# Two sets of accumulators by period, and one sum for three layers

## What is computed

```python
for i in range(3):
    z = jnp.einsum('bmd,bnd->bmnd', x, hidden).reshape(B, -1, D)
    cur = jnp.einsum('bcd,co->bod', z, Ws[i]) + bs[i][None, :, None]
    cur = jax.nn.relu(cur)                    # 200 rows a layer
    if i != 2:
        hidden, direct = cur[:, :100, :], cur[:, 100:, :]
    else:
        direct = cur
    finals.append(direct)
y = jnp.sum(jnp.concatenate(finals, axis=1), axis=-1)   # [512, 400], float32
```

## Time and profile before

| | before |
|---|---|
| time, median of 3 runs | 2781.72 us (2778.2 to 2781.84) |
| the profiled execution | 2781.59 us |
| its span, first to last instruction | 2779.8 us |
| PE, DVE, ACT busy | 97%, 97%, 63% of the span |
| mean granted clock of PE | 0.996 |
| one period | 21.10 us |

### The profile page before, as it was taken

The page is one execution under the profiler, slowest core; times in us unless marked ns, Lnnn a source line. Parts: engine busy times, 40 slices in busy tenths (PEclk is TensorE's granted clock), DMA queues, the critical chain, the costliest instruction groups (busy, mean ns, idle before and its releaser), DMA issues.

```text
span 2779.8 us, 52071 instructions
## 1 busy us (share of the span) xinstructions
PE 2702.4 (97%) x17960; PEld 2635.3 (95%) x17960; DVE 2710.3 (97%) x2725; ACT 1737.6 (63%) x2842; POOL 0.7 (0%) x7
## 2 busy tenths in 40 slices
PE   3899999999999999999999999999999999999998
PEld 3899999999999999999999999999999999999998
DVE  5999999999999999999999999999999999999998
ACT  3566666666666666666666666666666666666664
POOL 0000000000000000000000000000000000000000
PEclk9999999999999999999999999999999999999999
DMA  9454444444445444444444444444454444445442
GB/s 215 124 143 109 112 129 116 107 124 127 110 128 144 113 108 127 122 107 119 129 124 125 130 119 107 124 126 107 113 132 117 109 128 123 107 117 130 110 108 61
DMA packets 230994, 335.70 MB, mean 121 GB/s; under 512 B 28072, under 2 KB 165268, under 8 KB 230804
## 3 DMA queue, kind: packets, MB, share of 16 engines
q1 hardware_dynamic: 230902, 334.50, 46.2%
HBM read 329.71 MB, written 6.60 MB: 121 GB/s over the span
## 4 chain that ended last, share of the span: by engine, by line
PE 66%; DVE 18%; issue 13%; DMA 1%; DVEq 1%; SPq 1%; ACT 1%; ACTq 0%
PE acc L727 45%; PE acc L728 20%; DVE z_low L403 15%; DVE s L417 1%; DVE z L398 1%; DVE z L387 1%; DMA mixed<-in_L_rec_W_dram 0%; DVEq L401 0%; DMA x_right<-x_by_unit 0%; PE turned L740 0%; DVE direct L424 0%; DVE w_split L366 0%; DMA z<-w_rows_again 0%; DVEq L402 0%; ACT w_split L618 0%
## 5 line engine op out<-in xcount | busy, mean ns | idle before, releaser
L727 PE MATMUL acc<-w_split,z_high 128*128 128x400 f32 (+1 forms) x8832 | 2667.6, 369 | 67.7 <-DVE z_low L403 53.6
L728 PE MATMUL acc<-w_split,z_low 128*128 128x200 f32 (+1 forms) x8832 | 2253.1, 255 | 0.0
L727 PEld LDWEIGHTS acc<-w_split,z_high 128*128 128x128 f32 (+1 forms) x8832 | 1662.4, 188 | 134.2 <-DVE z_low L403 75.1
L583 ACT ACTIVATE z_high<-z 128x1024 fp32r<-128x1024 f32 (+2 forms) x1152 | 1182.1, 1026 | 888.1 <-DVE z L398 700.3
L728 PEld LDWEIGHTS acc<-w_split,z_low 128*128 128x128 f32 (+1 forms) x8832 | 1692.5, 192 | 0.0
L403 DVE TENSOR_TENSOR z_low<-z,z_high 128x1024 fp32r<-128x1024 f32 (+2 forms) x1152 | 1349.1, 1171 | 2.0 <-ACT z_high L583 1.4
L398 DVE TENSOR_TENSOR z<-mixed,xb 128x1024 f32<-128x1024 f32 (+1 forms) x1024 | 1210.3, 1182 | 3.7 <-ACT mixed L608 3.6
L608 ACT ACTIVATE mixed<-turned 32x128 f32<-32x128 f32 x768 | 204.7, 267 | 8.9
L605 ACT ACTIVATE mixed<-turned 96x512 f32<-96x512 f32 x256 | 150.7, 589 | 7.9 <-PE turned L740 3.0
L387 DVE TENSOR_TENSOR z<-x_left,x_right 118x896 f32<-118x896 f32 x128 | 138.8, 1084 | 2.0 <-DMA x_right<-x_by_unit 2.0
L424 DVE SCALAR_TENSOR_TENSOR direct<-s,direct 128x400 f32<-128x400 f32 (+2 forms) x133 | 72.7, 547 | 16.5
(11 more groups left out here) (26 smaller groups left out, 38.7 us busy)
## 6 DMA issues: line engine op xcount, KB each, us to landing
xb<-x_by_unit SPq DMA_DIRECT2D x384, 384.0 KB, 4.3
x_right<-x_by_unit SPq DMA_DIRECT2D x384, 136.5 KB
xb<-x_by_unit SPq DMA_DIRECT2D x384, 128.0 KB, 4.9
xb<-x_by_unit SPq DMA_DIRECT2D x128, 336.0 KB
xb<-x_by_unit SPq DMA_DIRECT2D x128, 84.0 KB
x_left<-x_by_unit SPq DMA_DIRECT2D x384, 19.5 KB
mixed<-in_L_rec_W_dram SPq DMA_DIRECT2D x5, 600.0 KB, 8.3
x_by_unit<-mixed SPq DMA_DIRECT2D x12, 160.0 KB, 3.0
```

What stands on the lines that cost most here:

```text
L583: nc.scalar.activation(z_high[slot % HIGH_RING][0:rows, 0:n * T], z[0:rows, slot % RING, 0:n * T], ACT.Copy).then_inc(high, 1)
L727: nc.tensor.matmul(a[:, 0:2 * O], z_high[slot % HIGH_RING][0:rows, tok], w, start=(c == 0), stop=False, skip_group_check=True)
L728: last = nc.tensor.matmul(a[:, 0:O], z_low[slot % RING][0:rows, tok], w[:, 0:O], start=False, stop=(c == chunks - 1), skip_group_check=True)
```

## The change

There are two sets of three accumulators, taken in turn by even and odd periods: six banks of PSUM where there were three. The bank for x's transposes goes down from three to one, so that x is transposed and copied in three parts, spread over blocks 1.1, 1.3 and 2.0 (in the first tile the odd set's three banks serve for it). `second_half2` and `sums2` are gone: `second_half` and `sums` take all three layers, 600 elements, and both stand in the next period, ACT's copy behind the high part of block 1.1 and DVE's sum behind the product of block 1.2. The adds are split in two, 200 elements each, since layer 2's results now lie elsewhere in `s`, and stand behind block 0's product. PE waits only for the sums of two periods ago, and the transposes stand behind block 1.0. `ident` has a place of its own.

```diff
 def layers_ended(r, d):

-    return (1, 2) if r == TILES - 1 and d >= D - 2 else (0, 2)
+    if (r, d) == (0, 0):
+        return 0, 2
+    if r == TILES - 1 and d >= D - 2:
+        return 1, (2 if d == D - 1 else 3)
+    return 0, 3
...
-        s = sb("s", [P, 4, 2, P])
+        s = sb("s", [P, 3, 2, P])
         half = sb("half", [P, 3, 2, HID])
-        ident = s[:, 2, 0, :]
+        ident = sb("ident", [P, P])[:, :]
         direct = sb("direct", [P, 4, HID])

-        acc = banks("acc", 3)
+
+        both = banks("acc", 6)
+        acc = [both[:, 0:3, :], both[:, 3:6, :]]
         turned = banks("turned", 1)
-        x_turned = banks("x_turned", X_BANKS)
+        x_turned = banks("x_turned", 1)
+
+        def x_part(r, part):
+            return acc[1][:, part, :] if r == 0 else x_turned[:, 0, :]
...
-            def sums(a, b, step, added):
+            def sums(a, b, par, step, added):

                 dve.wait_ge(half_in, step)
                 if added is not None:
                     dve.wait_ge(direct_in, added)
-                nc.vector.tensor_tensor(s[:, a:b, :, 0:HID], acc[:, a:b, 0:O].rearrange("p l (h o) -> p l h o", o=HID),
+                nc.vector.tensor_tensor(s[:, a:b, :, 0:HID],
+                                        acc[par][:, a:b, 0:O].rearrange("p l (h o) -> p l h o", o=HID),
                                         half[:, a:b, :, :], ALU.add).then_inc(s_in, 1)
...
-            def sums2(u):
-                dve.wait_ge(half2_in, u + 1)
-                dve.wait_ge(direct_in, u + 3)
-                nc.vector.tensor_tensor(s[:, 2:4, 1, 0:HID], acc[:, 2, 0:O].rearrange("p (h o) -> p h o", o=HID),
-                                        half[:, 2, :, :], ALU.add).then_inc(s2_in, 1)
+            def places(a, b):
+
+                return direct[:, a:b, :], (s[:, a:b, 1, 0:HID] if b <= 2 else s[:, 2, :, 0:HID])
...
                 dve.wait_ge(s_in, ended(n - 1))
                 dve.wait_ge(direct_in, n + 1)
-                if not (r == 0 and d == 1):
-                    dve.wait_ge(s2_in, n - 1)
...
                 else:
-                    add(0, 4).then_inc(direct_in, 1)
+                    add(0, 2)
+                    add(2, 4).then_inc(direct_in, 1)
...
                 product12(1, n, par, 1, base + 1, slot(1))
                 lows(base, slot(0), P, group_chunks(0))
-                if second:
-                    sums(0, 2, ended(0), 2)
                 product12(1, n, par, 2, base + 2, slot(2))
+                sums(last_a, last_b, 1 - par, ended(n - 1), n + 1)
                 lows(base + 1, slot(1), P, group_chunks(1))
                 product12(1, n, par, 3, base + 3, slot(3))
                 if second:
                     low_piece(7, 2, 2)
                 lows(base + 2, slot(2), P, group_chunks(2))
-                if not second:
-                    sums2(n - 2)
-                directs(r, d, n)
                 q = 4
                 if a == 0:
                     product0(n + 2, base + 4, slot(4))
+                directs(r, d, n)
+                if a == 0:
                     lows(base + 3, slot(3), P, group_chunks(3))
...
                 if final:
-                    sums(a, b, ended(n), n + 2)
+                    sums(a, b, par, ended(n), n + 2)
                 product12(2, n - 1, 1 - par, 3, base + q + 3, slot(q + 3))
                 lows(base + q + 2, slot(q + 2), P, group_chunks(2))
-                if not final:
-                    sums(a, b, ended(n), n + 2)
...
-            sums2(UNITS - 2)
+            dve.wait_ge(s_in, UNITS + 2)
+            dve.wait_ge(direct_in, UNITS + 1)
+            add(1, 2).then_inc(direct_in, 1)
...
                 product12(2, UNITS - 1, 1, g, at + g, at + g)
+                if g == 1:
+                    sums(2, 3, 1, UNITS + 3, None)
...
-            dve.wait_ge(s_in, ended(UNITS - 1))
-            dve.wait_ge(s2_in, UNITS - 1)
-            dve.wait_ge(direct_in, UNITS + 1)
-            add(1, 4).then_inc(direct_in, 1)
-            sums2(UNITS - 1)
-            dve.wait_ge(s2_in, UNITS)
+            dve.wait_ge(s_in, UNITS + 3)
             dve.wait_ge(direct_in, UNITS + 2)
+            add(2, 4).then_inc(direct_in, 1)
+            sums(2, 3, 0, UNITS + 4, UNITS + 3)
+            dve.wait_ge(s_in, UNITS + 4)
+            dve.wait_ge(direct_in, UNITS + 3)
             add(2, 4).then_inc(direct_in, 1)
...
-            def second_half(a, b, last):
+            def second_half(a, b, par, last):

                 act.wait_ge(freed, RING + last + 1)
-                nc.scalar.activation(half[:, a:b, :, :], acc[:, a:b, O:2 * O].rearrange("p l (h o) -> p l h o", o=HID), ACT.Copy)\
+                nc.scalar.activation(half[:, a:b, :, :], acc[par][:, a:b, O:2 * O].rearrange("p l (h o) -> p l h o", o=HID), ACT.Copy)\
                   .then_inc(half_in, 1)
-
-            def second_half2(last):
-                act.wait_ge(freed, RING + last + 1)
-                nc.scalar.activation(half[:, 2, :, :], acc[:, 2, O:2 * O].rearrange("p (h o) -> p h o", o=HID), ACT.Copy)\
-                  .then_inc(half2_in, 1)
...
                 highs(base, slot(0), P, group_chunks(0))
-                if second:
-                    second_half(0, 2, base - 1)
                 highs(base + 1, slot(1), P, group_chunks(1))
-                if second:
-                    dup(0, 2, ended(0))
+                second_half(last_a, last_b, 1 - par, base - 1)
                 highs(base + 2, slot(2), P, group_chunks(2))
+                if last_b > 2:
+                    dup(last_a, 2, ended(n - 1))
+                else:
+                    dup(0, 2, ended(n - 1))
...
-                else:
-                    second_half2(base - 1)
                 hidden(1, n - 1, 1 - par, ended(n - 1))
...
-                if not final:
+                if last_a == 0:
                     hidden(0, n + 1, 1 - par, ended(n - 1))
+                if turn:
+                    turned_x(r + 1, 0)
                 if second:
                     high_piece(2, 3)
                 highs(base + q, slot(q), P, group_chunks(0))
+                highs(base + q + 1, slot(q + 1), P, group_chunks(1))
                 if turn:
-                    for bank in range(X_BANKS):
-                        turned_x(r + 1, bank)
-                highs(base + q + 1, slot(q + 1), P, group_chunks(1))
+                    turned_x(r + 1, 1)
...
-                else:
-                    second_half(a, b, base + q - 1)
                 highs(base + q + 3, slot(q + 3), P, group_chunks(3))
-                if not final:
-                    dup(a, b, ended(n))
+                if turn:
+                    turned_x(r + 1, 2)
...
-            def turn_x(r):
+            def turn_x(r, part):
                 pe.wait_ge(x_in, 32 * (r + 1))
                 if r > 0:
-                    pe.wait_ge(xts_in, X_BANKS * r)
-                for k in range(BLOCKS):
-                    bank, j = k // X_PER_BANK, k % X_PER_BANK
-                    t = nc.tensor.transpose(x_turned[:, bank, j * T:(j + 1) * T], x_tile(r)[:, k * P:(k + 1) * P], ident)
-                    if j == X_PER_BANK - 1 or k == BLOCKS - 1:
-                        t.then_inc(x_turned_in, 1)
+                    pe.wait_ge(xts_in, X_PARTS * r + part)
+                for k in range(X_PER_BANK * part, min(BLOCKS, X_PER_BANK * (part + 1))):
+                    j = k % X_PER_BANK
+                    last = nc.tensor.transpose(x_part(r, part)[:, j * T:(j + 1) * T], x_tile(r)[:, k * P:(k + 1) * P], ident)
+                last.then_inc(x_turned_in, 1)
...

-                pe.wait_ge(s_in, ended(n - 1))
-                multiply(1, base, slot(0), 0)
-                multiply(1, base + 1, slot(1), 1)
-                if second:
-                    transpose(0, 2, ended(0))
-                if d == HEAD - 1 and r < TILES - 1:
-                    turn_x(r + 1)
-                multiply(1, base + 2, slot(2), 2)
-                multiply(1, base + 3, slot(3), 3)
+                pe.wait_ge(s_in, ended(n - 2))
+                multiply(1, par, base, slot(0), 0)
+                transpose(last_a, 2, ended(n - 1))
+                multiply(1, par, base + 1, slot(1), 1)
+                if turn:
+                    turn_x(r + 1, 0)
+                multiply(1, par, base + 2, slot(2), 2)
+                multiply(1, par, base + 3, slot(3), 3)
+                if turn:
+                    turn_x(r + 1, 1)
                 q = 4
                 if a == 0:
-                    multiply(0, base + 4, slot(4))
+                    multiply(0, par, base + 4, slot(4))
                     q = 5
-                if not second:
-                    pe.wait_ge(s2_in, n - 1)
...
                         transpose(a, b, ended(n))
-                    multiply(2, base + q + g, slot(q + g), g)
-                if not final:
-                    transpose(a, b, ended(n))
+                    multiply(2, par, base + q + g, slot(q + g), g)
```

(29 more changed lines are left out.)

51 lines of the change are left out of this document (30 added, 21 removed).

## The result

The kernel with the change takes 2788.01 us in the median (2785.64 to 2790.11), the kernel before 2781.72 in the runs beside it (2778.20 to 2784.64), eleven runs each. The ratio is 1.0024, with a 95% interval of 1.0015 to 1.0033: **0.24% slower, 6.3 us**. The forecast was 2797.5, 15.8 slower. The profiled execution took 2786.14, with a span of 2784.4.

The account below looks back on a forecast made before the run. DVE's own work was taken to bound the kernel at 21.10 us a period. The profiled 2781.6 plus 15.1 for 126 periods at 0.12 more, plus 0.9 once only, gave 2797.5 us, range 2777 to 2812.

Parts of the forecast that it names:

- What bounds the kernel: Steady state: DVE's own work fills the 21.10 us period; PE has some 0.7 us to spare; second accumulator set alone gives nothing.
- DVE's work: DVE's sums and adds: 1.46 us removed, 1.26 added, so 0.20 less, 20.90 us a period.
- The new wait: At the merged sum, DVE waits 0.28 us a period for ACT's 600-element copy, which waits for block 2.3's last matmul.
- the first pattern: Usual periods: the stretch from block 2.0's low part on DVE to PE's last matmul takes 10.61 us; sums lie 21.18 apart.
- I take 21.22, between the patterns: Period after the change, chosen between 21.18 and 21.25: 0.12 us more a period, bounds 0.08 and 0.21; 15.1 us over 126 periods.
- second pattern: In about a fifth of the periods block 2.0 starts later on PE; the stretch takes 10.68 us, the period 21.25.
- a wait against a count in a register: In the loop, ACT waiting so for a product starts 0.10 us after its end, not 0.04; might come on top.
- Once only: Outside the steady state: -1.1 us in the second period, +1.8 for three tile turns, +0.2 at the end; together +0.9.
- The rule that was set against the rows: About 125 ns DVE overhead per PSUM instruction: merged sum would cost 0.64 us, not 0.70, total some 8 us lower.
- The copy is there in time: Rival at the merged sum: ACT's copy lands by 1245.71, DVE never waits, the 0.20 is won: 2757 us; chance 0.13.
- No change that can be told: Rival at the merged sum: a wait of 0.16 to 0.24 us cancels the saving, 2776 to 2787 us; chance 0.11.
- PE late as well: Rival at PE's transposes: waiting for the tail-column copy or restarts moves PE's chain, period about 21.42, 2823 us; chance 0.11.

Follow-up runs that it names:

- ACT's line earlier: The kernel before with the adds on GpSimd, and ACT's relu in place one block earlier, behind the high part of block 2.0: 2832.09 us, ratio 1.0182.
- the copy apart: The changed kernel with layers 0 and 1 copied by ACT one block earlier, only layer 2's 200 elements at the old place, one merged sum: 2754.54 us, ratio 0.9904.

## Why the prediction was right in its direction and wrong in its size

**What bounds the kernel** was right: DVE's own work, with the second set of accumulators giving nothing by itself (a ratio of 1.0001), and PE below it with some 0.6 to spare (even at 20.88 another 0.40 less of DVE's work came off the period at once).

**DVE's work** was right: 0.70 for the merged sum as reckoned, 0.55 for the adds where 0.56 was reckoned, 20.88 instead of 20.90.

**The new wait** was right in place and cause. Each link came out close to the forecast of the first pattern:

| link | reckoned | measured |
|---|---|---|
| sum to block 2.0's low part | 9.81 | 9.80 |
| low part, PE's start | 1.27 | 1.27 |
| 31 pairs | 9.34 | 9.35 |
| ACT's start | 0.04 | 0.03 |
| copy of 600 | 0.69 | 0.67 |
| DVE's start | 0.03 | 0.03 |
| period | 21.18 | 21.15 |

**The step that failed is "I take 21.22, between the patterns".** The links gave 21.18 and the sum went on with 21.22, because a fifth of the periods of before had a second pattern at 21.25 and because a wait against a count in a register might cost 0.10 instead of 0.04. Neither came. The second pattern is not in the trace after: between the products of block 0 the distance is 21.15 or 21.16 nearly throughout, apart from the turns. In the trace before, it is PE that starts block 2.0 0.15 after its low part instead of 0.06, in 23 periods, and all of these are periods that are written out and not in the loop. There PE has a wait for layer 2's sum right ahead of block 2.0 (`s2_in`), and the change takes this wait away. The kernel with only the add moved keeps it and shows the pattern 23 times as well; the one with two sets alone has that wait ahead of block 1.0 and doesn't show it, though DVE's work sets its period too. That points to the wait, which the diff could have told, though no run changes it alone. The wait against a count in a register cost 0.03 (1246.63 + 0.26 to 1246.92), and the 0.10 that was read in the earlier trace rows was not its price. In the trace before, ACT starts a high part 0.03 to 0.04 after the product that it waits for in 552 of 644 cases in the loops, where the count is in a register, and 0.09 to 0.10 after it in 225 of 249 cases in the written-out periods, where it is a constant. Why it is the one or the other stays open. The term was taken at 0.12 a period and measured 0.05: of the 15.1 us some 6 to 7 were there. The lower bound, 0.08, was too high as well (the period is below the 21.18 to 21.31 that was to be seen): by 0.02 in the copy, and 0.01 over the other links together. One hundredth of a us in each period is 1.3 us of the total, and the forecast was the small difference between 0.28 of wait and 0.20 of saving. By the first pattern alone the forecast would have been 2781.6 + 0.08 x 126 + 0.9 = 2792.6; with the links as measured, 0.05, it would have been 2788.8, against 2788.0. The range, 2777 to 2812, took in the measured time.

**Once only.** The products of block 0, the fifth and the last, after:

```profile
107.98 1.08 DVE L396 TENSOR_TENSOR z<-x_left,x_right 118x896 f32<-118x896 f32 x1
...
2711.86 1.08 DVE L396 TENSOR_TENSOR z<-x_left,x_right 118x896 f32<-118x896 f32 x1
```

Before, the same two products lie at 110.87 and 2706.64. Up to the fifth, then, the kernel after is 2.9 ahead; from there to the last it loses 8.1; behind the last it gains 0.7 (the spans differ by the sum of the three, 2784.4 - 2779.8 = 4.6). Of the 8.1, three turns of a tile make 2.2: in each the wait ahead of the sum is 0.91 to 0.93 instead of 0.19, and the distance 21.88 to 21.90. The remaining 5.9 over 120 distances is the 0.05.

```profile
168.09 0.78 DVE L420 TENSOR_TENSOR s<-acc,half 128x600 f32<-128x600 f32 x1 [0.91 <-ACT half L598]
```

The turns were reckoned at 0.6 each and are 0.73. At the start -1.1 was reckoned; in the second period DVE's wait did shrink from 2.50 to 1.29:

```profile
74.74 0.57 DVE L420 TENSOR_TENSOR s<-acc,half 128x400 f32<-128x400 f32 x1 [1.29 <-ACT half L598]
```

The rest of the 2.9 can't be put down to the change: other kernels above that keep the two sums are also ahead there in their profiled executions (two sets alone: 1.1; the add moved alone: 2.5; the adds on GpSimd: 0.3, and 2.8 with ACT's line earlier). It looks like a spread of the start between executions, which no run here tests.

**The rule that was set against the rows.** Fusing two sums into one saved DVE 0.06 a period (0.48 + 0.28 - 0.70), as the rows of before had said. The Trainium skill gives DVE some 125 ns of overhead for an instruction on PSUM (Perfetto Trace Analysis, Optimizing Scalar/DVE Operations). These traces don't agree with it: half of that was saved. The other rule of the Trainium skill's section is that breaking instructions up may let work be completed sooner. It was the one that mattered, and the runs put a price and a condition on it: broken up with one part moved ahead, 33 us less than the changed kernel; broken up in place, 9 us more.

**The rivals.** "The copy is there in time" gave 2757, and the two kernels that made it so (the copy apart, the sum later) measured 2754.5 and 2754.3: its sum was right, its condition wasn't met by 0.27. "No change that can be told" named a wait of 0.16 to 0.24 and was nearer in size than the forecast: it was 0.27 of wait against 0.22 of saving, and 2788.0 lies 1 us above the 2787 at which that rival ended. "PE late as well" did not come; the kernel with the sum one place later shows its first signs at no cost.

## What to carry to other kernels

Before fusing instructions on the bottleneck engine, take each input's ready time against the moment at which the engine comes to the fused instruction: it waits for the latest input, and if that input depends on the engine's own earlier output, the wait repeats in every period and makes a ring that a few hundredths on a half-idle engine lengthen. Ask first what the saving consists of: here nearly all of it was an instruction waiting for the result of the one right ahead, and moving one line behind independent work gave 29 us without any of the rest.

## What the runs showed of the hardware

A 400-element fp32 add on GpSimd took 4.85 us beside a DVE that works without a pause, and 6.41 us when started earlier. Both times it ended 0.9 us after DVE stopped, and DVE's instructions kept their usual 1.22. Once it took 1.61 us, and then a DVE instruction took 2.08 instead of 1.22. An engine at 0% is thus no free engine next to a full DVE: moving 0.49 us of work to it cost 1.0 us of waiting. An instruction that waits for the result of the one right ahead of it cost DVE 0.21 to 0.22 us more than the same pair with one other instruction in between. ACT started 0.03 us after the matmul that it waited for, DVE 0.03 after ACT's copy, and PE 0.05 after DVE's low part. Behind a product, ACT started after either 0.03 to 0.04 or 0.09 to 0.10.
